# One decoder layer on one core: the order of its pieces dealt anew, ten halves by C on DVE, the first gate behind its softplus

## The chip, the cores and the metric

The kernel runs on one core of a Trainium2 chip. The metric is the device time of one execution in microseconds (us). Engines: PE (TensorE), DVE (VectorE), ACT (ScalarE), POOL (GpSimd) and SP (SyncE), which here only issues DMAs.

## The reference

32 sequences of 256 tokens of width 256 go through three blocks, each with a residual and a layer norm behind it.

```
# 1: state space block, d_inner 512, 16 states, scan restarts every 64 tokens
xc, res = split(x @ W_in.T + b_in)
u = silu(causal_conv3(xc) + conv_b)
dlt, Bm, Cm = split(u @ W_x.T)
delta = softplus(dlt @ W_dt.T + b_dt)
h[t] = exp(delta * A)[t] * h[t-1] + (delta * Bm * u)[t]     # per channel and state
y = sum over states of h * Cm
x = layernorm(x + (y * silu(res)) @ W_out.T + b_out)
# 2: cross attention, 16 heads of 16, keys and values from ctx_1024
x = layernorm(x + softmax(q k^T / 4) v @ w_o.T + b_o)
# 3: eight experts with fixed tokens (32 of each sequence to each)
x = layernorm(x + (silu(x @ w1) * (x @ w3)) @ w2)
```

Everything is float32.

## The kernel before

Blocks 1 and 2 run as one software pipeline over the 32 batches (sequences), block 3 follows over the eight experts. The change touches only the pipeline.

Each engine has a list of pieces (offset, function) which `run_steps` unrolls. An iteration has 16 slots. A piece with offset o runs for batch c in iteration c + o // 16, slot o % 16; within one slot the order is that of the list. So the offset says on each engine where a piece stands among the others, and the list says it only among pieces of one slot. There is no planner at run time: each engine executes its instructions in this order and waits on semaphores. SP's list is the order in which DMAs are issued, all on one queue; a wait of one holds up all behind it.

What happens to a batch:
- conv(m) and gate_proj(m), m = 0 to 3, on PE from xT. ACT evacuates (conv_evac, gate_evac), then in `silu` loads the table of Silu, makes u and the gate, and loads the table of Exp and Ln again.
- x_proj on PE gives delta's low-rank input and B and C, which xp_evac and bc_store put to DRAM; SP's bc_load replicates B and C over the partitions. dt_proj and ACT's softplus give delta. POOL's w_piece multiplies u by delta.
- SP's delta_store and w_store put both in DRAM, and replicate(part), part = 0 to 3, brings four tiles each of both back, replicated (8 DMAs of 128 KB). replicate(0) waits for both stores.
- The scan works in 16 tiles of 128 partitions x 4 states x 256 tokens. For tile t POOL makes dBu (L506, three buffers), ACT the decays in two halves of two states (L582, three PSUM banks), DVE scans each half (L764), and the states are multiplied by C: most by POOL in `h` (L516), the halves listed in HC_DVE by DVE. For these the scan is written to the PSUM bank, DVE's hC_piece multiplies it into h (L777), and clear_starts zeroes the first column of the bank (L787); only then is the half counted as scanned, which frees the bank for ACT and, for half 1, dBu's buffer for POOL.
- PE's state_sum(m) sums four tiles, DVE's gating multiplies by the gate, out_proj and residual(0) and norm(0) end block 1.
- Attention: k, q and v projections; `high` (ACT) and `low` (DVE) split q and k in two parts, store_parts stores them, load_stack(gr) reads them back stacked for four heads (eight DMAs of 64 KB in pieces of 1 KB, and a small one). scores, row_max (L829), max_transpose, scores_T, softmax_exp, pv and so on follow, one head a slot.

At the start SP loads the convolution's weights and the rows of biases; DVE multiplies both out (six products for w_conv, L733), casts the rows to `bias` (L738) and corrects them (L742). Then xT of batch 0 and ten weights are loaded; after the first of them SP waits until DVE is done. gate_proj(0) of the first batch waits for all ten.

Of the kernel before, what the change touches and what calls it, by code (L numbers as in the profile page):

```python
# [10 lines left out]
ALU = mybir.AluOpType  # L11
ACT = mybir.ActivationFunctionType
# [32 lines left out]
HC_DVE = [(1, 0), (1, 1), (4, 1), (5, 0), (5, 1), (6, 1), (8, 0), (9, 1), (10, 0), (10, 1), (14, 1)]  # L45
# [148 lines left out]
def mixers(nc, io, x2_dram, scratch, shared):  # L194
# [3 lines left out]
    with ExitStack() as ctx:  # L198
# [75 lines left out]
        def scores_T_bank(n):  # L274
# [4 lines left out]
        s_const = sem("weights_loaded")  # L279
        s_const_p = sem("const_set_pool")  # L280
# [49 lines left out]
        N_CONV = 6 + NDA + TAPS * KD  # L330
# [7 lines left out]
        def _(sp):  # L338
            sp.dma_start(w_xc.rearrange("p q t -> p (q t)"), io["w_xc"]).then_inc(s_conv_ld, 16)
            sp.dma_start(conv_rows, io["conv_rows"].partition_broadcast(P)).then_inc(s_conv_ld, 16)  # L340
            for tile, name in bias_parts:
                sp.dma_start(tile, io[name]).then_inc(s_bias_ld, 16)
# [107 lines left out]
            def store_x2T(b):  # L450
# [5 lines left out]
            run_steps([  # L456
                (O_K - 2, load_ctx),
                (O_Q + 3, store_parts(q_dram, s_q_hi, s_q_lo, s_q_dram)),
                (O_REP + 13, replicate(3)),
                *[(O_LD + 11 + 6 * e, load_expert(e, shared.load_w13)) for e in range(2)],  # L460
                *[(O_LD + 14 + 6 * e, load_expert(e, shared.load_w2)) for e in range(2)],
                (O_LD + 23, load_tokens),
                (O_K + 5, store_parts(k_dram, s_k_hi, s_k_lo, s_k_dram)),
                (O_SP + 2, w_store),
                (O_OUT, load_x_tok),
                (0 + 1, load_x),
                (O_SP + 2, delta_store),
                (O_XP + 2, bc_load),
                (O_REP + 1, replicate(0)),
                (O_REP + 7, replicate(2)),  # L470
                *[(O_LD + HG * gr - 2, load_stack(gr)) for gr in range(NG)],
                (O_X2T + 3, load_columns),
# [10 lines left out]
        @block.gpsimd  # L483
        def _(pool):
            nc.gpsimd.memset(k_st[4 * DK:SK].bitcast(F32), 0.0).then_inc(s_const_p, 1)
            pool.wait_ge(s_const_p, 1)
            nc.gpsimd.memset(q_st[4 * DK:SK].bitcast(F32), 0.0).then_inc(s_const_p, 1)
            pool.wait_ge(s_const_p, 2)
            nc.gpsimd.memset(v[:], 1.0).then_inc(s_const_p, 1)
            pool.wait_ge(s_const_p, 3)  # L490
            nc.gpsimd.memset(k_st[4 * DK:4 * DK + 2].bitcast(F32), 1.0).then_inc(s_const_p, 1)
            pool.wait_ge(s_const_v, N_SET)

            def w_piece(b):
# [25 lines left out]
            run_steps([  # L520
                *[(O_SCAN + t - 1, dBu_piece(t)) for t in range(NU)],
                (O_SP + 2, w_piece),
                *[(O_SCAN + t + 1, hC_piece(t)) for t in HC_POOL],
            ], B)

        @block.scalar
        def _(act):

            nc.scalar.preload_act_table_set(EXP_LN)
            act.wait_ge(s_bias_ld, 16 * len(bias_parts))  # L530
            nc.scalar.activation(a_neg[:], a_neg[:], ACT.Exp).then_inc(s_const_a, 1)
# [16 lines left out]

            def silu(b):
                act.wait_ge(s_conv, b.value(2, 2))  # L550
                nc.scalar.activation(u[:], u[:], ACT.Silu).then_inc(s_u, 1)
                act.wait_ge(s_gate, b.value(2, 2))
                nc.scalar.activation(gate[:, b.par], gate[:, b.par], ACT.Silu).then_inc(s_gsilu, 1)
                nc.scalar.preload_act_table_set(EXP_LN)

# [136 lines left out]
            def max_load(gr):  # L692
# [11 lines left out]
                *[(O_GATE + 4 * half + 2, gate_evac(half)) for half in range(2)],  # L704
                (O_K + 1, high(s_k_mm, s_k_hi, s_q_dram, 1)),
                (O_N2 + 3, store_x2),
                *[(O_SCAN + t - 1, decay(t, 0)) for t in range(NU)],
                *[(O_MT + HG * gr + 2, max_store(gr)) for gr in range(NG)],
                *[(O_MT + HG * gr + 3, max_load(gr)) for gr in range(NG)],
# [7 lines left out]
                (O_Q + 1, high(s_q_mm, s_q_hi, s_k_dram, 0)),  # L717
# [7 lines left out]
        def _(dve):  # L725
            nc.vector.memset(xT[:, :, 0:TAPS - 1], 0.0).then_inc(s_const_v, 1)
            nc.vector.memset(eps, EPS).then_inc(s_const_v, 1)
            for i in range(NDA):
                nc.vector.memset(dA[i][:], 0.0).then_inc(s_const_v, 1)
            dve.wait_ge(s_conv_ld, 32)  # L730
# [4 lines left out]
            dve.wait_ge(s_bias_ld, 16 * len(bias_parts))  # L735
            nc.vector.tensor_tensor(rows, rows, row_scales, ALU.mult).then_inc(s_const_v, 1)
            dve.wait_ge(s_const_v, N_CONV - 3)
            nc.vector.tensor_copy(bias[:], rows).then_inc(s_const_v, 1)  # L738
            dve.wait_ge(s_const_v, N_CONV - 2)

# [5 lines left out]
            dve.wait_ge(s_const_a, 1)  # L746
# [112 lines left out]
            def x1T_evac(b):  # L859
# [7 lines left out]
                (O_OF + 1, residual(1, s_of_mm, a_ps, s_r2, s_st2, s_mv2, s_ln2, s_x1, TT)),  # L867
# [3 lines left out]
                *[(O_ON + HG * gr + 1, head_norm(gr)) for gr in range(NG)],  # L871
                *[(O_SCAN + t, scan(t, 1)) for t in range(NU)],
# [9 lines left out]
        def _(pe):  # L882
# [20 lines left out]
            def gate_proj(m):  # L903
                def piece(b):
                    pe.wait_ge(s_xT, b.value(16, 16))
                    if m == 0 and not b.back(1):
                        pe.wait_ge(s_const, 16 * N_WEIGHTS)
                        pe.wait_ge(s_const_v, N_SET)
                        pe.wait_ge(s_const_p, 4)
                    if m % 2 == 0:  # L910
                        bank_f.wait_read(pe)
                        mm(f_ps[:], bias[32:36, m // 2 * P:(m // 2 + 1) * P], bias[32:36, BC:], True, False)
                    for k in range(KD):
                        i = mm(f_ps[:, m % 2], w_gate[:, k, m * P:(m + 1) * P], xT[:, k, TAPS - 1:], False,
                               m % 2 == 1 and k == KD - 1)
                    i.then_inc(s_gate_mm, 1)
                    bank_f.read_by(s_gate, 2, b, m // 2 + 1)
                return piece

            def x_proj(b):  # L920
                pe.wait_ge(s_u, b.value(1, 1))
# [16 lines left out]
            def state_sum(m):  # L938
                def piece(b):
                    n = b.value(NU, 4 * m)  # L940
                    pe.wait_ge(s_hC, b.value(len(HC_POOL), sum(t < 4 * m + 4 for t in HC_POOL)))
# [148 lines left out]
            def attn_out(tt):  # L1090
# [17 lines left out]
                *[(O_GATE + 4 * (m // 2), gate_proj(m)) for m in range(ND)],  # L1108
                (O_X1T, transpose(x_of, s_x1, TT, s_x1T_mm, s_x1T, bank_a, a_ps)),
                *[(O_DT, dt_proj(m)) for m in range(ND)],  # L1110
                *[(O_V, v_proj(tt)) for tt in range(TT)],
                *[(O_OF, attn_out(tt)) for tt in range(TT)],
# [318 lines left out]
```

## Time and profile before

| | |
|---|---|
| three runs | 2794.74 us median (2792.72 to 2795.35) |
| profiled execution | 2792.28 us, span 2790.5 us, mean granted clock of TensorE 0.955 |
| PE busy | 2424.6 us (87%) |
| DVE busy | 2140.0 us (77%) |
| POOL busy | 2074.5 us (74%), all of it in the pipeline of blocks 1 and 2 |
| ACT busy | 1802.9 us (65%) |
| DMA | 399.65 MB, mean 143 GB/s |

The span runs from the first to the last instruction. Busy shares are over the whole span; the pipeline ends at some 2270 us, so an engine's share there is higher. POOL has nothing to do in the last quarter.

### The profile page before, as it was taken

What the parts mean: (1) busy time and instruction counts of PE and PEld (TensorE: products, weight loads), DVE (VectorE), ACT (ScalarE), POOL (GpSimd) and SP (SyncE); (2) the same over time, 40 slices, a digit from 0 to 9 for tenths busy, and PEclk for the clock granted to TensorE, in tenths of its full rate; (3) what the DMA queues carried; (4) which work ended last, traced back from release to release, by engine and by line L of the source; (5) the groups of instructions that cost most, each with busy time, mean ns of one, the idle gap of its engine ahead of it and who ended that gap; (6) DMA issues with size and microseconds to landing.
All of it is one profiled execution on the core that took longest, in us unless ns stands there. A gap on an engine that the chain in (4) does not pass through costs nothing. (4 is left out here: it accounts for less than half of the span.)

```text
span 2790.5 us, 49779 instructions
## 1 busy us (share of the span) xinstructions
PE 2424.6 (87%) x14816; PEld 1660.6 (60%) x14816; DVE 2140.0 (77%) x3586; ACT 1802.9 (65%) x3972; POOL 2074.5 (74%) x968
## 2 busy tenths in 40 slices
PE   3578888888889898889889888898888879999998
PEld 2345666666666666666666666666665545555554
DVE  1778999999999999999999999999999832322332
ACT  1666777877888888777877787878777541211111
POOL 2999999999999999999999999999999500000000
PEclk8788999999999999999999999999998879999999
DMA  3456566666666666666666666666666360343221
GB/s 118 128 133 149 150 165 168 165 158 157 157 169 166 160 158 165 165 162 168 166 169 164 162 164 166 165 173 163 166 172 158 86 180 12 91 126 96 78 79 31
DMA packets 319323, 399.65 MB, mean 143 GB/s; under 512 B 115697, under 2 KB 256241, under 8 KB 314962
## 3 DMA queue, kind: packets, MB, share of 16 engines
q1 hardware_dynamic: 303698, 384.91, 53.5%
q10 hardware_dynamic: 15360, 11.55, 1.5%
q8 instruction: 124, 2.03, 0.3%
q14 instruction: 141, 1.16, 0.2%
HBM read 300.86 MB, written 94.37 MB: 142 GB/s over the span
## 5 line engine op out<-in xcount | busy, mean ns | idle before, releaser
L506 POOL TENSOR_TENSOR arena<-arena 128x1024 f32<-128x1024 f32 x512 | 1208.2, 2363 | 66.6 <-DMA arena<-w_dram 42.3
L582 ACT ACTIVATE dA_ps<-arena,a_neg 128x252 f32<-128x252 f32 x2048 | 868.7, 461 | 330.4 <-DVE dA_ps L787 172.0
L764 DVE TENSOR_TENSOR_SCAN arena<-dA_ps,arena 128x512 f32<-128x512 f32 x672 | 803.6, 1208 | 112.5 <-ACT dA_ps L582 88.0
L516 POOL TENSOR_TENSOR arena<-arena 128x1024 f32<-128x1024 f32 (+1 forms) x416 | 808.1, 1943 | 17.8 <-DVE arena L764 17.2
L764 DVE TENSOR_TENSOR_SCAN dA_ps<-dA_ps,arena 128x512 f32<-128x512 f32 x352 | 416.2, 1205 | 3.9 <-POOL arena L506 3.7
L887 PE MATMUL a_ps<-xT,w_conv 128*128 128x256 f32 x1536 | 369.8, 391 | 0.0
L829 DVE TENSOR_REDUCE mx<-s_ps 128x2 f32<-128x512 f32 x497 | 334.0, 672 | 23.2 <-PE s_ps L887 23.2
L887 PEld LDWEIGHTS a_ps<-xT,w_conv 128*128 128x128 f32 x1536 | 288.4, 194 | 54.1 <-issue 16.5
L887 PE MATMUL y_ps<-arena,sel 128*32 128x256 f32 x4096 | 257.5, 393 | 55.5 <-DVE m_rows L835 27.8
L640 ACT ACTIVATE probs<-st_ps 128x512 f32<-128x512 f32 x493 | 285.3, 579 | 29.7 <-PE st_ps L887 25.5
L887 PE MATMUL s_ps<-k_st,q_st 96*128 96x256 f32 x994 | 260.6, 344 | 43.7 <-DVE mx L829 28.0
L887 PE MATMUL st_ps<-q_st,k_st 96*128 96x256 f32 x986 | 221.9, 307 | 51.5 <-ACT probs L640 41.8
L777 DVE TENSOR_TENSOR arena<-dA_ps,arena 128x512 f32<-128x512 f32 x352 | 230.9, 677 | 4.4
L887 PEld LDWEIGHTS st_ps<-q_st,k_st 96*128 96x128 f32 x986 | 154.1, 194 | 120.1 <-issue 100.3
L887 PEld LDWEIGHTS s_ps<-k_st,q_st 96*128 96x128 f32 x994 | 166.7, 197 | 98.0 <-issue 59.4
L887 PEld LDWEIGHTS y_ps<-arena,sel 128*32 128x32 f32 x4096 | 127.9, 112 | 144.2 <-POOL arena L516 64.9
L1240 DVE TENSOR_TENSOR hT<-silu,u_ps 128x512 f32<-128x512 f32 x80 | 55.0, 688 | 193.7 <-PE u_ps L1311 160.9
L887 PE MATMUL a_ps<-bias 2*128 2x512 f32 (+2 forms) x192 | 93.3, 486 | 117.4 <-DVE parts L819 38.4
L1213 ACT ACTIVATE silu<-g_ps 128x512 f32<-128x512 f32 (+1 forms) x96 | 56.5, 596 | 210.0 <-PE g_ps L1311 209.9
L1311 PE MATMUL g_ps<-arena 128*128 128x512 f32 x384 | 181.7, 599 | 3.1 <-PEq L198 3.1
L1311 PE MATMUL u_ps<-arena 128*128 128x512 f32 x320 | 150.5, 592 | 0.0
L1329 PE MATMUL d_ps<-arena,hT 128*128 128x256 f32 x640 | 145.9, 383 | 0.0
(111 smaller groups left out, 3272.9 us busy)
## 6 DMA issues: line engine op xcount, KB each, us to landing
arena<-delta_dram SPq DMA_DIRECT2D x512, 128.0 KB, 2.8
arena<-w_dram SPq DMA_DIRECT2D x512, 128.0 KB, 3.2
arena<-bc_dram SPq DMA_DIRECT2D x128, 256.0 KB, 4.5
q_st<-q_parts_dram SPq DMA_DIRECT2D x512, 64.0 KB
k_st<-k_parts_dram SPq DMA_DIRECT2D x512, 64.0 KB
w_dram<-u SPq DMA_DIRECT2D x32, 512.0 KB, 2.8
delta_dram<-delta SPq DMA_DIRECT2D x32, 512.0 KB, 3.8
k_parts_dram<-parts SPq DMA_DIRECT2D x32, 512.0 KB, 4.0
```

Source lines behind the costliest of these rows:

```text
L506: pool.tensor_tensor(dBu[:, n % NB], w_r[:, n // RP % 2, t % RP].unsqueeze(1).to_broadcast([P, QS, L]), bc_r[:, b.par, 0], ALU.mult).then_ ...
L516: pool.tensor_tensor(h[:, n % NH, states], h[:, n % NH, states], bc_r[:, b.par, 1, states], ALU.mult).then_inc(s_hC, 1)
L582: last = nc.scalar.activation(dA[n % NDA][:, q, :, 1:], delta_r[:, n // (2 * RP) % 2, t % RP].rearrange("p (c t) -> p c t", t=CH)[:, :, 1: ...
L640: nc.scalar.activation(probs[:, n % NPROB], scores_T_bank(n), ACT.Exp, scale=float(DK) ** -0.5).then_inc(s_exp, 1)
L764: nc.vector.tensor_tensor_scan(dst, decays, dBu[:, n % NB, 2 * half:2 * half + 2].rearrange("p q t -> p (q t)"), 0.0, ALU.mult, ALU.add).t ...
L777: nc.vector.tensor_tensor(h[:, n % NH, 2 * half:2 * half + 2], state[:].rearrange("p q c t -> p q (c t)"), bc_r[:, b.par, 1, 2 * half:2 * ...
L829: nc.vector.tensor_reduce(mx[:, hd], scores_bank(b.value(H, hd)), AX.X, ALU.max).then_inc(s_max, 1)
L887: return nc.tensor.matmul(out, lhsT, rhs, start=first, stop=last)
L1213: nc.scalar.activation(dst, g_ps[i % 2][first:last], ACT.Silu).then_inc(f_silu, 1)
L1240: nc.vector.tensor_tensor(hT[first:last, i // 2, HALF * (i % 2):HALF * (i % 2 + 1)], silu[first:last, i % 2], ups[first:last], ALU.mult).t ...
L1311: ins = nc.tensor.matmul(ps[i % 2][:], w13[:, b.par, k, col:col + P], x2T[:, b.par, k, cols], start=(k == 0), stop=(k == KD - 1))
L1329: nc.tensor.matmul(d_ps[(2 * t + i) % ND_PS][:, 0:D], hT[:, k, tokens], w2[:, b.par, k], start=(k == 0), stop=False)
```

## The change

- HC_DVE has ten halves instead of eleven: tiles 1, 2, 4, 5, 6, 8, 9 and 14 with half 1, tile 10 with both. Before: tiles 1, 5 and 10 with both, 4, 6, 9 and 14 with half 1, 8 with half 0. So POOL has 15 pieces by C a batch, 8 of them of half a tile, instead of 13 with 5.
- The first batch's gate projections, their evacuation and silu come behind its softplus (offset O_SP + 2).
- Set-up: the rows of biases are loaded first, ACT converts them to `bias` instead of DVE, DVE does the six products behind the rows. Three weights (w_x, w_dt, w_gate) are loaded at once, with a semaphore of their own; x_proj of the first batch waits for these, and state_sum(0) for the others.
- The lists of SP, POOL, ACT, DVE and PE are ordered anew, and some offsets change by one.

```diff
-HC_DVE = [(1, 0), (1, 1), (4, 1), (5, 0), (5, 1), (6, 1), (8, 0), (9, 1), (10, 0), (10, 1), (14, 1)]
+HC_DVE = [(1, 1), (2, 1), (4, 1), (5, 1), (6, 1), (8, 1), (9, 1), (10, 0), (10, 1), (14, 1)]
...
+        front_weights = [(w_x[:], "w_x"), (w_dt[:], "w_dt"), (w_gate[:], "w_gate")]
         weights = [
-            (w_gate[:], "w_gate"), (w_x[:], "w_x"), (w_dt[:], "w_dt"), (sel[:], "sel"), (w_out[:], "w_out"),
+            (sel[:], "sel"), (w_out[:], "w_out"),
...
             def load_weights():
+                for tile, name in front_weights:
+                    sp.dma_start(tile, io[name]).then_inc(s_front, 16)
+                sp.wait_ge(s_const_v, N_SET)
                 for tile, name in weights:
                     sp.dma_start(tile, io[name]).then_inc(s_const, 16)
-                    sp.wait_ge(s_const_v, N_SET)
...
+                (O_REP + 13, replicate(3)),
+                *[(O_LD + 11 + 6 * e - 1, load_expert(e, shared.load_w13)) for e in range(2)],
+                *[(O_LD + 14 + 6 * e - 2, load_expert(e, shared.load_w2)) for e in range(2)],
+                (O_LD + 23, load_tokens),
+                (O_REP + 7, replicate(2)),
+                (O_K + 5, store_parts(k_dram, s_k_hi, s_k_lo, s_k_dram)),
                 (O_K - 2, load_ctx),
+                (O_SP + 2, delta_store),
                 (O_Q + 3, store_parts(q_dram, s_q_hi, s_q_lo, s_q_dram)),
...
-                (O_OUT, load_x_tok),
+                (O_OUT - 1, load_x_tok),
+                (O_X2T + 4, load_columns),
+                (0 + 1, load_x),
+                (O_XP + 2, bc_load),
                 (O_SP + 2, w_store),
                 (O_REP + 1, replicate(0)),
-                *[(O_LD + HG * gr - 2, load_stack(gr)) for gr in range(NG)],
+                *[(O_LD + HG * gr - 1, load_stack(gr)) for gr in range(NG)],
...
+            act.wait_ge(s_const_v, N_ROWS)
+            nc.scalar.activation(bias[:], rows, ACT.Copy).then_inc(s_const_a, 1)
...
+            def silu_gate(b):
+                act.wait_ge(s_gate, b.value(2, 2))
+                nc.scalar.activation(gate[:, b.par], gate[:, b.par], ACT.Silu).then_inc(s_gsilu, 1)
+
             def silu(b):
                 act.wait_ge(s_conv, b.value(2, 2))
                 nc.scalar.activation(u[:], u[:], ACT.Silu).then_inc(s_u, 1)
-                act.wait_ge(s_gate, b.value(2, 2))
-                nc.scalar.activation(gate[:, b.par], gate[:, b.par], ACT.Silu).then_inc(s_gsilu, 1)
+                if b.back(1):
+                    silu_gate(b)
                 nc.scalar.preload_act_table_set(EXP_LN)
+
+            def first_gate(b):
+                if not b.back(1):
+                    for half in range(2):
+                        gate_evac(half)(b)
+                    silu_gate(b)
+                    nc.scalar.preload_act_table_set(EXP_LN)
...
+                (O_SP + 2, first_gate),
...
-                (O_N2, norm(1, s_mv2, s_ln2, s_x2)),
+                (O_N2 - 1, norm(1, s_mv2, s_ln2, s_x2)),
...
-                (O_Q + 1, high(s_q_mm, s_q_hi, s_k_dram, 0)),
+                (O_Q, high(s_q_mm, s_q_hi, s_k_dram, 0)),
...
                 *[(O_SCAN + t, scan(t, 1)) for t in range(NU)],
+                *[(O_S + hd + 1, row_max(hd)) for hd in range(H)],
+                (O_Q + 1, low(s_q_hi, s_q_lo)),
                 *[(O_SCAN + t, hC_piece(t, half)) for t, half in HC_DVE],
-                *[(O_S + hd + 1, row_max(hd)) for hd in range(H)],
...
-                (O_Q + 1, low(s_q_hi, s_q_lo)),
...
-                    if m == 0 and not b.back(1):
-                        pe.wait_ge(s_const, 16 * N_WEIGHTS)
-                        pe.wait_ge(s_const_v, N_SET)
-                        pe.wait_ge(s_const_p, 4)
...
+            def first_gate(b):
+                if not b.back(1):
+                    for m in range(ND):
+                        gate_proj(m)(b)
...
             def x_proj(b):
+                if not b.back(1):
+                    pe.wait_ge(s_front, 16 * len(front_weights))
+                    pe.wait_ge(s_const_v, N_SET)
...
+                (O_SP + 2, first_gate),
```

## Rows read from the trace of the kernel before

**Rows 1.** Busy time of POOL in the second batch and in 28 later ones.
```profile
115.00:180.00 65.00, 63.64 (x30) 0.78 0.38 111
245.00:2119.00 1874.00, 1805.39 (x841) 0.98 0.65 164
```

**Rows 2.** Timeline of POOL: w_piece of batch 3 and of batch 31 (start, length).
```profile
245.39 2.36 POOL L497 TENSOR_TENSOR u<-u,delta 128x1024 f32<-128x1024 f32 x1 [0.29 <-ACT delta L572]
...
2119.09 2.35 POOL L497 TENSOR_TENSOR u<-u,delta 128x1024 f32<-128x1024 f32 x1 [0.16 <-ACT delta L572]
```

**Rows 3.** Groups of POOL's instructions in 245:2119 us (busy, mean ns, idle before).
```profile
L506 POOL TENSOR_TENSOR arena<-arena 128x1024 f32<-128x1024 f32 x449 | 1059.7, 2363 | 48.3 <-DMA arena<-w_dram 28.7 <-DVE dA_ps L787 18.7
L516 POOL TENSOR_TENSOR arena<-arena 128x1024 f32<-128x1024 f32 x224 | 529.2, 2362 | 15.8 <-DVE arena L764 15.2
L516 POOL TENSOR_TENSOR arena<-arena 128x512 f32<-128x512 f32 x140 | 177.9, 1270 | 0.0
```

**Rows 4.** Timeline of SP's queue of DMA issues in one steady batch.
```profile
770.22 0.36 SPq L419 DMA_DIRECT2D q_st<-q_parts_dram  x1
...
773.90 0.59 SPq L421 DMA_DIRECT2D q_st<-k_st  x1
...
780.38 1.74 SPq L363 DMA_DIRECT2D arena<-bc_dram  x4
...
784.80 0.34 SPq L371 DMA_DIRECT2D w_dram<-u  x1
...
789.49 0.33 SPq L398 DMA_DIRECT2D ctxT<-in_ctxT  x1
...
790.58 2.33 SPq L386 DMA_DIRECT2D arena<-delta_dram  x4
```

**Rows 5.** Timeline of ACT in that batch: first decay of the next.
```profile
799.50 1.66 ACT L582 ACTIVATE dA_ps<-arena,a_neg 128x252 f32<-128x252 f32 x4 [0.28 <-DMA arena<-w_dram]
```

**Rows 6.** Stretches of that batch; last three columns: granted clock, DMA share, GB/s.
```profile
772.00:781.00 9.00, 7.45 (x65) 4.94 (x56) 7.80 (x13) 8.76 (x17) 8.72 (x6) 1.00 0.47 62
781.00:786.00 5.00, 4.00 (x10) 2.96 (x11) 4.34 (x8) 4.96 (x10) 4.84 (x3) 0.66 0.99 211
786.00:789.00 3.00, 2.76 (x15) 2.19 (x14) 2.63 (x5) 2.38 (x6) 2.01 (x2) 1.00 0.91 339
789.00:791.00 2.00, 2.00 (x23) 1.37 (x25) 2.00 (x3) 1.56 (x5) 2.00 (x2) 1.00 0.33 53
793.00:798.00 5.00, 4.92 (x46) 3.40 (x39) 4.97 (x7) 4.44 (x12) 5.00 (x3) 1.00 1.01 238
```

**Rows 7.** Groups of DVE's instructions in 245:2119 us.
```profile
L777 DVE TENSOR_TENSOR arena<-dA_ps,arena 128x512 f32<-128x512 f32 x309 | 202.6, 676 | 3.8
L804 DVE TENSOR_TENSOR x_tok<-a_ps,x_tok 128x512 f32<-128x512 f32 x55 | 37.4, 680 | 37.5 <-PE a_ps L887 37.5
L787 DVE MEMSET dA_ps<- 128x8 f32 x308 | 15.2, 65 | 0.4
```

**Rows 8.** Timeline of all engines over the front.
```profile
15.73 5.49 PE L887 MATMUL a_ps<-xT,w_conv 128*128 128x256 f32 x12
...
30.93 0.76 PE L887 MATMUL f_ps<-bias 4*128 4x512 f32 x1 [9.71 <-issue]
...
35.12 2.76 PE L887 MATMUL a_ps<-xT,w_conv 128*128 128x256 f32 x12
...
46.88 0.60 ACT L538 ACTIVATE u<-a_ps 128x512 f32<-128x512 f32 x1 [2.00 <-PE a_ps L887]
...
49.75 1.04 ACT L553 ACTIVATE gate<-gate 128x1024 f32<-128x1024 f32 x1
...
59.10 0.43 SPq L367 DMA_DIRECT2D delta_dram<-delta  x1
...
64.33 1.71 SPq L386 DMA_DIRECT2D arena<-delta_dram  x4
...
70.61 2.45 ACT L582 ACTIVATE dA_ps<-arena,a_neg 128x252 f32<-128x252 f32 x6 [13.09 <-DMA arena<-w_dram]
```

More of the change, by code:

```diff
@@ L279, in mixers @@
         s_const = sem("weights_loaded")
+        s_front = sem("front_weights_loaded")
         s_const_p = sem("const_set_pool")
@@ L329, in mixers @@
         N_WEIGHTS = len(weights)
-        N_CONV = 6 + NDA + TAPS * KD
+        N_ROWS = 3 + NDA
+        N_CONV = 5 + NDA + TAPS * KD
         N_SET = N_CONV + 2
@@ L338, in _ @@
         def _(sp):
+            for tile, name in bias_parts:
+                sp.dma_start(tile, io[name]).then_inc(s_bias_ld, 16)
             sp.dma_start(w_xc.rearrange("p q t -> p (q t)"), io["w_xc"]).then_inc(s_conv_ld, 16)
             sp.dma_start(conv_rows, io["conv_rows"].partition_broadcast(P)).then_inc(s_conv_ld, 16)
-            for tile, name in bias_parts:
-                sp.dma_start(tile, io[name]).then_inc(s_bias_ld, 16)
             def load_weights():
+                for tile, name in front_weights:
+                    sp.dma_start(tile, io[name]).then_inc(s_front, 16)
+                sp.wait_ge(s_const_v, N_SET)
                 for tile, name in weights:
                     sp.dma_start(tile, io[name]).then_inc(s_const, 16)
-                    sp.wait_ge(s_const_v, N_SET)
                 sp.wait_ge(s_const_p, 4)
@@ L521, in _ @@
                 *[(O_SCAN + t - 1, dBu_piece(t)) for t in range(NU)],
+                *[(O_SCAN + t + 1, hC_piece(t)) for t in HC_POOL],
                 (O_SP + 2, w_piece),
-                *[(O_SCAN + t + 1, hC_piece(t)) for t in HC_POOL],
             ], B)
@@ L551, in silu, with later_gate_evac, piece @@
                 nc.scalar.activation(u[:], u[:], ACT.Silu).then_inc(s_u, 1)
-                act.wait_ge(s_gate, b.value(2, 2))
-                nc.scalar.activation(gate[:, b.par], gate[:, b.par], ACT.Silu).then_inc(s_gsilu, 1)
+                if b.back(1):
+                    silu_gate(b)
                 nc.scalar.preload_act_table_set(EXP_LN)
+            def first_gate(b):
[4 more added lines that the diff above has]
+                    nc.scalar.preload_act_table_set(EXP_LN)
+            def later_gate_evac(half):
+                def piece(b):
+                    if b.back(1):
+                        gate_evac(half)(b)
+                return piece
             def xp_evac(b):
@@ L703, in _ @@
                 (O_SILU, silu),
-                *[(O_GATE + 4 * half + 2, gate_evac(half)) for half in range(2)],
+                *[(O_GATE + 4 * half + 2, later_gate_evac(half)) for half in range(2)],
                 (O_K + 1, high(s_k_mm, s_k_hi, s_q_dram, 1)),
@@ L707, in _ @@
                 *[(O_SCAN + t - 1, decay(t, 0)) for t in range(NU)],
+                (O_SP + 2, first_gate),
+                *[(O_MT + HG * gr + 3, max_load(gr)) for gr in range(NG)],
                 *[(O_MT + HG * gr + 2, max_store(gr)) for gr in range(NG)],
-                *[(O_MT + HG * gr + 3, max_load(gr)) for gr in range(NG)],
                 (O_XP + 1, xp_evac),
                 *[(O_MT + HG * gr + 1, max_high(gr)) for gr in range(NG)],
-                (O_N2, norm(1, s_mv2, s_ln2, s_x2)),
+                (O_N2 - 1, norm(1, s_mv2, s_ln2, s_x2)),
                 *[(O_CONV + 4 * half + 3, conv_evac(half)) for half in range(2)],
@@ L729, in _ @@
                 nc.vector.memset(dA[i][:], 0.0).then_inc(s_const_v, 1)
+            dve.wait_ge(s_bias_ld, 16 * len(bias_parts))
+            nc.vector.tensor_tensor(rows, rows, row_scales, ALU.mult).then_inc(s_const_v, 1)
             dve.wait_ge(s_conv_ld, 32)
@@ L734, in _ @@
                                             conv_rows[:, tap * DI:(tap + 1) * DI], ALU.mult).then_inc(s_const_v, 1)
[L735 to L739, printed above, removed]
+            dve.wait_ge(s_const_a, 1)
             for first, last, cols in ((0, 96, BC), (96, P, 2 * BC)):
@@ L866, in _ @@
                 *[(O_SCAN + t, scan(t, 0)) for t in range(NU)],
-                (O_OF + 1, residual(1, s_of_mm, a_ps, s_r2, s_st2, s_mv2, s_ln2, s_x1, TT)),
                 (O_X1T + 1, x1T_evac),
@@ L918, in gate_proj, with later_gate, piece @@
                 return piece
+            def first_gate(b):
+                if not b.back(1):
+                    for m in range(ND):
+                        gate_proj(m)(b)
+            def later_gate(m):
+                def piece(b):
+                    if b.back(1):
+                        gate_proj(m)(b)
+                return piece
             def x_proj(b):
+                if not b.back(1):
+                    pe.wait_ge(s_front, 16 * len(front_weights))
+                    pe.wait_ge(s_const_v, N_SET)
                 pe.wait_ge(s_u, b.value(1, 1))
@@ L940, in piece @@
                     n = b.value(NU, 4 * m)
+                    if m == 0 and not b.back(1):
+                        pe.wait_ge(s_const, 16 * N_WEIGHTS)
+                        pe.wait_ge(s_const_p, 4)
                     pe.wait_ge(s_hC, b.value(len(HC_POOL), sum(t < 4 * m + 4 for t in HC_POOL)))
@@ L1107, in _ @@
                 *[(O_CONV + 2 * m, conv(m)) for m in range(ND)],
-                *[(O_GATE + 4 * (m // 2), gate_proj(m)) for m in range(ND)],
+                *[(O_GATE + 4 * (m // 2), later_gate(m)) for m in range(ND)],
+                (O_SP + 2, first_gate),
                 (O_X1T, transpose(x_of, s_x1, TT, s_x1T_mm, s_x1T, bank_a, a_ps)),
+                *[(O_OF, attn_out(tt)) for tt in range(TT)],
                 *[(O_DT, dt_proj(m)) for m in range(ND)],
                 *[(O_V, v_proj(tt)) for tt in range(TT)],
-                *[(O_OF, attn_out(tt)) for tt in range(TT)],
                 *[(O_OUT, out_proj(tt)) for tt in range(TT)],
```

13 lines of the change are left out of this document (2 added, 11 removed).

## The prediction

> **What bounds the kernel now.** I read the stretches of POOL first, then its groups with what ended their idle time, then SP's own queue, then the stretches by DMA share, and last the front. The w_piece of batch 3 starts at 245.39 and that of batch 31 at 2119.09 [rows 2]: 28 cycles of 66.92 us. POOL is busy 1805.39 of that stretch [rows 1], 64.48 us a cycle, so it idles 2.44. The reader should see in [rows 3] that 28.7 us of this idle time end with the landing of arena<-w_dram (1.0 a cycle), 18.7 with DVE's clearing of a bank (0.7) and 15.2 with a DVE scan (0.5). The first is the one that matters: it is the replication of delta and w for the first four tiles of a batch, replicate(0), and ACT's first decay waits for the same landing [rows 5]. So the cycle is a loop: landing of replicate(0), then POOL, ACT, DVE and PE with little slack for three quarters of a batch, softplus, w on POOL, the two stores, replicate(0), landing.
>
> The last part of the loop lies in SP's queue and is full of DMA. In the batch shown, stack(3) is issued from 770.22 to 774.49, SP then waits, bc_load goes at 780.38, w_store at 784.80, load_ctx at 789.49 (it waited for v_proj), replicate(0) at 790.58 [rows 4], and it has landed at 799.5 [rows 5]. The DMA engines are only 0.47 busy from 772 to 781, when stack(3) runs by itself at 62 GB/s. Then the share is 0.99 (bc), 0.91 (stores), 0.33, and 1.01 (replication) [rows 6]. Before bc_load there is room; behind it there is nearly none. The columns also show that a pure byte count misleads: the same 16 engines move 339/0.91 = 373 GB/s of busy time in the stores and 62/0.47 = 132 in the stack loads.
>
> **The change part by part.**
>
> *Order on each engine.* A piece's place is its offset modulo 16, then its place in the list. Only pieces of one slot can swap by the list. Going through the lists, on PE nothing swaps except the first batch's gate. On POOL only the length of hC pieces changes. On ACT norm(1) moves from slot 2 to 1, and the high part of q from 12 to 11. On DVE row_max and the low part of q go ahead of the hC pieces. On SP three orders change: bc_load now comes ahead of stack(3) (slots 11 and 11, before 11 and 10), delta_store ahead of w_store, and k's store behind replicate(2). So most of "dealt anew" is the same order written otherwise.
>
> *Ten halves instead of eleven.* POOL before: 8 full pieces and 5 halves a batch; after: 7 full and 8 halves (only tile 10 is wholly DVE's). That is 3 x 1.27 - 2.36 = +1.45 us by the means of [rows 3], +1.4 because successive instructions overlap by a few hundredths. POOL's own work becomes 64.5 + 1.4 = 65.9, which leaves 1.0 under the present cycle. It can take the place of the waits for DVE (1.2 a cycle), but not of the wait for the landing, behind which it begins. DVE loses one product and one clear: 0.68 + 0.07 = 0.74 us a batch [rows 7]. The other moves, (1,0) to (2,1) and (8,0) to (8,1), are the same work elsewhere. The clearing of half 1 frees dBu's buffer and of half 0 only a bank, so two tiles more hold dBu until DVE's product is done: between 0 and 2 x 0.68 = 1.4 for POOL. I take 0, as dBu waits for a bank only 0.7 a cycle in all.
>
> *bc_load ahead of stack(3).* This is the step I charge. stack(3) is nine DMAs, 4.3 us to issue [rows 4], and 0.47 x 9 = 4.2 us of all DMA engines [rows 6]. They move from the empty stretch to between bc_load and the stores. bc has its data until 786; the stack then takes until 790.2; the stores need 0.91 x 3 = 2.7 and a little, so they end at 793.1, not at about 789.3. ctx and q's store, issued while SP waits, take some 2.2 more (791 to 793 now), and the bulk of replicate(0), now 793 to 798, becomes 795.3 to 800.3: 2.3 later. From both sides: nothing, if bc_load comes earlier by as much or the landing was not the last thing awaited; 4.2, if none of the gaps fills. The gaps from 781 to 793 hold 0.05 + 0.27 + 1.34 = 1.7, of which the blocks above use nearly all, so I stay at 2.3. Queued behind on SP are delta_store, w_store, ctx, q's store and replicate(0); for the last POOL and ACT wait, and through decay(0) DVE. stack(3) itself, needed by the scores of head 12, lands as they start; its bound is 0 to 1 us of PE, and I take 0.
>
> As measured, the stack's 1 KB pieces cost the DMA engines 4.2 us for 0.5 MB. By the Trainium skill, "DMA: Bandwidth & Descriptors", section "Why small descriptors are slow (HBM only)", a packet has a fixed cost of about 3 cycles beside one per 32 bytes, which for 1 KB is 35 instead of 32, a tenth. By that rule the 0.5 MB would need an estimated 1.6 us at the stores' rate and would fit the gaps, which is the first rival below. The trace does not agree: 132 GB/s is far from a tenth below 373.
>
> *delta_store ahead of w_store.* In the steady batches it is issued behind the stack now and wins nothing. In the front it does (below).
>
> *The moves that I price together.* DVE's row maxima come up to 0.68 or 1.35 us sooner in nine slots. PE's maximum transposes wait for them, PE's out_proj follows, and DVE waits 37.5/28 = 1.3 a cycle for out_proj [rows 7]. Bounds 0 and 1.3; I take 0.3, a quarter, as only the group in that slot is on this path. norm(1) one slot earlier makes ACT wait for moments before a decay, q's high part earlier delays one exponential by 0.6; both fall where ACT waits for DVE anyway. Cost 0, bounds -0.5 to +0.6 a cycle.
>
> *The front.* Now PE stops after the first convolution block, because the first gate projection waits for all ten weights until 30.93 [rows 8]. After the change conv runs on: block 0 ends at 21.2 (its cold 5.49), block 1 takes 2.76 to 3.2, the evacuation and the bias product 1.4, blocks 2 and 3 5.6, so the second evacuation starts at 31.2 instead of 46.88: 15.7 less. The reordering of DVE's and ACT's set-up leaves PE's start where it is: the six products (3.7 us) now come last instead of the conversion, bounds -1 and +1, I take 0. delta_store no longer waits for w: both stores now start at 58.7 and 59.10, and replicate(0) goes at 64.33 [rows 8]; with delta gone 2.9 earlier the last landing comes 1.7 sooner. Bounds 0 and 2.9. Sum of the front -17.4. The gate that is put behind softplus costs PE about 5 us and ACT 0.6 x 2 + 1.3 + 1.04 + 1.3 = 4.8; they are covered by the 13.09 us in which ACT awaits the replication [rows 8]. Without that cover it would cost some 5.
>
> **The sum,** against the profiled execution's own 2792.28 (span 2790.5; it lies 2.46 under the median of the three runs, 2794.74):
> front -17.4; cycles 1 to 3, in which POOL's 30 instructions fill 63.64 of 65 us [rows 1] and no stack is loaded yet, 3 x 1.4 = +4.2; 28 cycles x (2.3 - 0.74 - 0.3) = 28 x 1.25 = +35.0. Together +21.8: 2814.1, and on the scale of the median 2816.5.
>
> **Rivals.**
> *The DMA shift is hidden, and the front decides (faster).* Place: replicate(0)'s landing. If stack(3) costs the loop less than about 0.6, the cycle is paced by POOL's 65.9 and what DVE still makes it wait, 66.5 say. For it: the landing is late by only 1.0 in the mean, and the batch has slack where bc_load waits for its store. Against: POOL, ACT and DVE all hang on that landing. Time: -17.4 + 4.2 - 28 x 0.4 = -24.4, so 2770. It decides from where the steady cycle grows by less than 0.27.
> *Break even.* The same with a cycle longer by 0.27 to 0.67, about 2795.
> *Both costs in full.* The stack takes its 4.2 and POOL's 1.4 isn't absorbed but for half: 28 x (4.2 - 0.74 + 0.7) = +116, less 13: 2897.
> *The front doesn't come.* Should the first gate or the weights end later than the replication, up to 5 of the 17.4 go; it stays inside the range of each case.
>
> **Chances.** Forecast 0.51 (its own range 2803 to 2850), hidden 0.29, break even 0.12, both in full 0.08. What a measurement of this kernel can tell from no change is about 0.2%, 5.6 us. Faster 0.29, same 0.12, slower 0.59. The range reaches down to the hidden case and leaves out most of the last: 2768 to 2862.
>
> **What would show it.** replicate(0) issued some 13 us behind bc_load instead of 10.2; stack(3) between bc_load and the stores; POOL's and ACT's wait for arena<-w_dram at 2 to 3 us a cycle while POOL's waits for DVE shrink; cycles of w_piece near 68.2; the first softplus some 16 us earlier. If the cycles are 66.9 or less the step on the DMA is wrong. If ACT's first decay isn't near 53, the front is.

## The result, and the profile after

The changed kernel takes 2828.29 us (median of 4 runs, 2825.39 to 2832.81) against 2795.05 for the kernel before in the same comparison. The ratio is 1.012, 95% interval 1.0102 to 1.0138. The profiled execution took 2826.22, against 2792.28: +33.9, where the forecast had +21.8.

The page's span line, then POOL in the two stretches of [rows 1] (us, busy and instructions, granted clock, DMA share, GB/s):

```profile
span 2824.4 us, 49751 instructions
```

```profile
115.00:180.00 65.00, 65.00 (x33) 0.84 0.45 128
245.00:2119.00 1874.00, 1808.74 (x882) 0.97 0.66 161
```

In the second batch's 65 us POOL now has no idle moment: its added work took the place of the 1.36 us that it idled there before. The w_piece of batch 3 and of batch 31, to be set beside [rows 2]:

```profile
231.93 2.34 POOL L502 TENSOR_TENSOR u<-u,delta 128x1024 f32<-128x1024 f32 x1
...
2137.63 2.37 POOL L502 TENSOR_TENSOR u<-u,delta 128x1024 f32<-128x1024 f32 x1 [0.25 <-ACT delta L596]
```

28 cycles of (2137.63 - 231.93)/28 = 68.06 us instead of 66.92. So the +33.9 divide as follows. The w_piece of batch 3 is 13.5 earlier, the 28 cycles are 32.0 longer, and from the w_piece of batch 31 to the end of the span 686.8 us pass instead of 671.4, 15.4 more.

POOL's groups in 245:2119 us, the answer to [rows 3]:

```profile
L511 POOL TENSOR_TENSOR arena<-arena 128x1024 f32<-128x1024 f32 x441 | 1041.7, 2362 | 58.8 <-DMA arena<-w_dram 57.3 <-DVE dA_ps L810 1.3
L521 POOL TENSOR_TENSOR arena<-arena 128x1024 f32<-128x1024 f32 x193 | 456.4, 2365 | 6.0 <-DVE arena L787 5.7
L521 POOL TENSOR_TENSOR arena<-arena 128x512 f32<-128x512 f32 x221 | 281.8, 1275 | 0.0
```

The waits for DVE (18.7 and 15.2) are down to 1.3 and 5.7; the wait for the landing of replicate(0) is up from 28.7 to 57.3, two us a cycle. POOL's own work is 1808.74 in 27.5 cycles, 65.7 instead of 64.5.

SP's issues in one steady batch, as in [rows 4], and ACT's first decay of the next batch, as in [rows 5]:

```profile
1046.60 2.50 SPq L368 DMA_DIRECT2D arena<-bc_dram  x4
...
1049.21 0.36 SPq L424 DMA_DIRECT2D q_st<-q_parts_dram  x1
...
1053.10 0.59 SPq L426 DMA_DIRECT2D q_st<-k_st  x1
...
1053.88 0.35 SPq L372 DMA_DIRECT2D delta_dram<-delta  x1
...
1054.41 0.34 SPq L376 DMA_DIRECT2D w_dram<-u  x1
...
1056.99 0.33 SPq L403 DMA_DIRECT2D ctxT<-in_ctxT  x1
...
1060.21 1.74 SPq L391 DMA_DIRECT2D arena<-delta_dram  x4
```

```profile
1067.28 1.66 ACT L606 ACTIVATE dA_ps<-arena,a_neg 128x252 f32<-128x252 f32 x4 [0.17 <-DMA arena<-w_dram]
```

stack(3) (1049.21 to 1053.69) stands between bc_load and the stores, and replicate(0) goes 13.6 us behind bc_load instead of 10.2; in the mean of the 30 batches from the third on it is 13.5 instead of 10.9. The stretches of that batch, as in [rows 6] (last columns: granted clock, DMA share, GB/s):

```profile
1038.00:1047.00 9.00, 7.44 (x73) 5.11 (x72) 7.81 (x13) 8.75 (x18) 9.00 (x5) 1.00 0.03 7
1047.00:1052.00 5.00, 3.64 (x19) 2.73 (x17) 4.59 (x9) 4.96 (x8) 5.00 (x4) 1.00 0.76 205
1052.00:1056.00 4.00, 2.56 (x10) 1.99 (x11) 3.96 (x7) 3.36 (x9) 3.94 (x3) 0.94 1.12 138
1056.00:1060.00 4.00, 4.00 (x28) 2.53 (x26) 2.99 (x5) 3.06 (x8) 4.00 (x3) 0.64 1.01 346
1062.00:1067.00 5.00, 4.88 (x33) 3.68 (x25) 5.00 (x8) 3.67 (x9) 4.07 (x2) 1.00 0.97 230
```

The stretch ahead of bc_load, 0.47 busy before, is now empty (0.03), and from 1052 to 1067 the DMA engines are hardly ever free. The four us from 1052 to 1056 belong almost wholly to stack(3), fully busy at 138 GB/s. (The share adds up the times of all packets; over 1.00, packets of one engine overlap.)

The front, as in [rows 8]:

```profile
16.10 7.97 PE L910 MATMUL a_ps<-xT,w_conv 128*128 128x256 f32 x24
...
25.25 5.45 PE L910 MATMUL a_ps<-xT,w_conv 128*128 128x256 f32 x24
...
30.73 0.60 ACT L545 ACTIVATE u<-a_ps 128x512 f32<-128x512 f32 x1 [6.02 <-PE a_ps L910]
...
41.85 0.34 SPq L372 DMA_DIRECT2D delta_dram<-delta  x1
...
42.66 3.78 PE L910 MATMUL f_ps<-xT,w_gate 128*128 128x256 f32 x8
...
47.96 2.79 SPq L391 DMA_DIRECT2D arena<-delta_dram  x4
...
53.64 1.06 ACT L558 ACTIVATE gate<-gate 128x1024 f32<-128x1024 f32 x1
...
56.01 2.45 ACT L606 ACTIVATE dA_ps<-arena,a_neg 128x252 f32<-128x252 f32 x6
```

The four convolution blocks run through, the second evacuation starts at 30.73 (46.88), and the decays start at 56.01 (70.61).

Four waits of the steady stretch (who waited for whom: us in total, times, longest). In the kernel before they were 7.1, 5.6, 37.5 and 11.1 us, so the first, second and fourth have grown much and the third little:

```profile
ACT rstd L616 <- DVE mean_var L836: 70.5, 54, 2.7
PE s_ps L910 <- DMA q_st<-k_st: 24.6, 27, 2.4
DVE x_tok L827 <- PE a_ps L910: 43.0, 28, 2.0
DVE mx L852 <- PE s_ps L910: 33.6, 36, 2.0
```

And the end of SP's queue in the pipeline, where the weights of expert 0 (L182) are now issued between the last two stack loads:

```profile
2275.47 0.59 SPq L426 DMA_DIRECT2D q_st<-k_st  x1
...
2276.10 2.05 SPq L182 DMA_DIRECT2D arena<-in_w  x4
...
2278.26 0.40 SPq L424 DMA_DIRECT2D q_st<-q_parts_dram  x1
...
2281.98 0.59 SPq L426 DMA_DIRECT2D q_st<-k_st  x1
```

### The profile page after: what moved, and what is told of

It reads as the page before. It is cut to its first block, busy times and chain, and to the rows that moved or that the text cites. A ratio compares the mean times of both kernels' runs of the same rounds, so it can differ in the third digit from the quotient of the medians.

```text
span 2824.4 us, 49751 instructions
## 1 busy us (share of the span) xinstructions
PE 2432.1 (86%) x14816; PEld 1675.6 (59%) x14816; DVE 2126.4 (75%) x3521; ACT 1813.5 (64%) x3975; POOL 2114.2 (75%) x1032
## 4 chain that ended last, share of the span: by engine, by line
POOL 37%; PE 29%; issue 16%; SPq 5%; DVE 5%; DMA 5%; ACT 2%; ACTq 0%; DVEq 0%; POOLq 0%
POOL arena L511 20%; POOL arena L521 17%; PE a_ps L910 7%; PE g_ps L1348 6%; PE d_ps L1366 5%; PE u_ps L1348 5%; SPq L424 2%; PE f_ps L910 2%; SPq L391 1%; DMA w_dram<-u 1%; PE y_ps L910 1%; DVE arena L787 1%; ACT dA_ps L606 1%; DVE mx L852 1%; DVE dA_ps L787 1%
## 5 line engine op out<-in xcount | busy, mean ns | idle before, releaser
L787 DVE TENSOR_TENSOR_SCAN arena<-dA_ps,arena 128x512 f32<-128x512 f32 x704 | 846.1, 1211 | 113.3 <-POOL arena L511 45.7
L521 POOL TENSOR_TENSOR arena<-arena 128x512 f32<-128x512 f32 (+1 forms) x480 | 855.4, 1782 | 8.1 <-DVE arena L787 7.6
L787 DVE TENSOR_TENSOR_SCAN dA_ps<-dA_ps,arena 128x512 f32<-128x512 f32 x320 | 383.8, 1208 | 4.5 <-ACT dA_ps L606 2.0
L910 PEld LDWEIGHTS a_ps<-xT,w_conv 128*128 128x128 f32 x1536 | 289.4, 194 | 54.6 <-issue 16.5
L800 DVE TENSOR_TENSOR arena<-dA_ps,arena 128x512 f32<-128x512 f32 x320 | 214.5, 679 | 0.6
```

The source lines that it names most:

```text
L787: nc.vector.tensor_tensor_scan(dst, decays, dBu[:, n % NB, 2 * half:2 * half + 2].rearrange("p q t -> p (q t)"), 0.0, ALU.mult, ALU.add).t ...
L800: nc.vector.tensor_tensor(h[:, n % NH, 2 * half:2 * half + 2], state[:].rearrange("p q c t -> p q (c t)"), bc_r[:, b.par, 1, 2 * half:2 * ...
L910: return nc.tensor.matmul(out, lhsT, rhs, start=first, stop=last)
```

## The experiments

Each is a kernel of its own, timed over five rounds beside the kernel before on the same chip. The kernel before had medians of 2794.6, 2793.0 and 2792.2 in the three comparisons. The last four kernels below were timed in the third comparison and are set against kernels of the second; by the ratios their differences come out 1 to 3 us larger than by the medians. "Cycle" is the mean distance of w_piece from batch 3 to batch 31, "tail" the time from the last w_piece to the end of the span, both in the profiled execution. That is a single one, up to 12.7 us from the median of its kernel, so cycles that differ by 0.1 or 0.2 tell nothing.

**The stack loads back ahead of bc_load, in the changed kernel.**

```diff
-                *[(O_LD + HG * gr - 1, load_stack(gr)) for gr in range(NG)],
+                *[(O_LD + HG * gr - 2, load_stack(gr)) for gr in range(NG)],
```

> The changed kernel with the stack loads at their old offset, so that stack(3) is issued ahead of bc_load again; all else as changed, the tail's order too. Theory (moved DMA): replicate(0) comes some 10 us behind bc_load again instead of 13.6, POOL's wait for arena<-w_dram falls from 2.0 to about 1 us a cycle, the cycle from 68.06 to 66.7 and the time by 28 x 1.4 = 38 to about 2790. Rival (POOL's 1.4 us of added work is what costs): cycle stays above 67.6 and the time above 2815.

Measured: 2809.77, ratio 1.0046 (1.0025 to 1.0068), cycle 67.44, tail 682.9. Half of what was expected: 18 us come back, and 0.6 of the cycle. The rival is not confirmed either. replicate(0) goes 11.5 us behind bc_load in the mean, and POOL waits 39.2 us for its landing. Something else in the lists cost the rest: the kernel with ACT's new list alone (below) has the same cycle, 67.43.

**The experts' weights later, in the changed kernel.**

```diff
-                *[(O_LD + 11 + 6 * e - 1, load_expert(e, shared.load_w13)) for e in range(2)],
-                *[(O_LD + 14 + 6 * e - 2, load_expert(e, shared.load_w2)) for e in range(2)],
+                *[(O_LD + 12 + 6 * e, load_expert(e, shared.load_w13)) for e in range(2)],
+                *[(O_LD + 14 + 6 * e, load_expert(e, shared.load_w2)) for e in range(2)],
```

> The changed kernel with the expert weights' loads moved behind the last batch's stack(3) in SP's queue (slot 12 instead of 10). Theory (tail): in the changed kernel w1 and w3 of expert 0 are issued ahead of the last batch's stack(3) and from w_piece of batch 31 to the end 686.8 us pass instead of 671.4; here about 672, time 15 lower, about 2813; cycles unchanged at 68.1. Rival (the longer tail comes from the other orders or from the norm's place): the time stays within 4 of 2828.

Measured: 2830.20, ratio 1.0117 (1.0089 to 1.0144). The tail is 676.5, 10.3 shorter, but the cycle is 68.44 in the profile, though nothing of a steady batch was changed. The time is what the rival said, the tail two thirds of what the theory said, and the cycles of this execution scatter from 66.9 to 70.7 us. Inconclusive, and tried again below in the faster kernel.

**Ten halves only, in the kernel before** (the new HC_DVE and nothing else).

> The kernel before with the ten halves only. Theory: POOL's 1.4 us a batch are absorbed by its waits for DVE (1.2 a cycle), DVE has 0.74 less, so the cycle stays within 0.3 of 66.9 and the time within 10 of 2795, rather above for the first three cycles (+4). Rival (POOL is the bound): 28 x 1.4 + 4 = +43, about 2838.

Measured: 2782.79, ratio 0.9953 (0.9935 to 0.9971), cycle 66.30. Better than either theory, and the sign is against the small loss that the first expected. POOL's largest group in this kernel:

```profile
L506 POOL TENSOR_TENSOR arena<-arena 128x1024 f32<-128x1024 f32 x453 | 1075.5, 2374 | 14.9 <-DMA arena<-w_dram 13.4 <-DVE dA_ps L787 1.3
```

Its wait for DVE's clearing is nearly gone (18.7 to 1.3), and half of the wait for the landing too (28.7 to 13.4). Fourteen of its 28 cycles behind batch 3 last between 65.6 and 65.9, and POOL's own work is 65.7 a cycle; in the kernel before none fell below 65.9.

**The front only, in the kernel before** (set-up, first gate behind softplus; lists and halves as before).

> The kernel before with the new set-up and the first gate behind its softplus, and nothing else. Theory: first w_piece at 42.0 instead of 56.4, all behind it unchanged: 14 less, about 2781. Rival (the start is given back in the first cycles, as the pipeline then stands in another phase): less than 6 saved.

Measured: 2778.64, ratio 0.9934 (0.9910 to 0.9958), first w_piece at 40.76, cycle 66.89, tail 672.1. The 16 us are kept to the end.

**Halves and front together, all lists as before.**

> The changed kernel with all five lists as before (the first gate's entries added): ten halves and the new front, nothing of the new orders. Theory (the orders alone cost): the gains of the front (-16) and of the ten halves (-12) add, about 2767, cycle 66.3. Rival (with the front the pipeline stands in another phase and the gains don't add): 2778 or more.

Measured: 2762.62, ratio 0.9881 (0.9856 to 0.9905), cycle 66.42, tail 672.5. The gains add (0.9953 x 0.9934 = 0.9887). So the new lists alone turn 2763 into 2828. Of these, the lists of PE and POOL leave the order within every slot as it was, so SP's, ACT's and DVE's are what is left.

The next three put one new list each on this kernel.

**DVE's new list.**

```diff
-                *[(O_SCAN + t, hC_piece(t, half)) for t, half in HC_DVE],
                 *[(O_S + hd + 1, row_max(hd)) for hd in range(H)],
+                (O_Q + 1, low(s_q_hi, s_q_lo)),
+                *[(O_SCAN + t, hC_piece(t, half)) for t, half in HC_DVE],
```

> As the kernel with halves and front only, plus the changed list of DVE (row_max and q's low part ahead of the products by C, residual(1) behind head_norm). Theory (ACT's list is the second culprit): cycle within 0.3 of 66.3, time within 8 of the kernel with halves and front only. Rival (the products put later hold the banks and POOL's states): +1 a cycle, +28.

(residual(1) moves in the list too, but neither it nor the low part of q passes another piece of its slot; only the row maxima really moved.)

Measured: 2755.61, ratio 0.9856 (0.9830 to 0.9881), cycle 66.22. That is 7 us below the kernel without it in the same comparison, with overlapping intervals, so the gain is not clear of noise. It has the lowest median of the study, well below the kernel before and the changed one.

**ACT's new list.**

```diff
-                (O_N2, norm(1, s_mv2, s_ln2, s_x2)),
+                (O_N2 - 1, norm(1, s_mv2, s_ln2, s_x2)),
...
-                (O_Q + 1, high(s_q_mm, s_q_hi, s_k_dram, 0)),
+                (O_Q, high(s_q_mm, s_q_hi, s_k_dram, 0)),
```

> As the kernel with halves and front only, plus the changed list of ACT (norm(1) in slot 1, q's high part in slot 11). Theory: norm(1) makes ACT wait for the moments some 2.5 us a cycle as in the changed kernel (70.5 us in all), with decays and exponentials queued behind it; cycle up by about 1.1 to 67.4, time +30. Rival (ACT has that slack, as its waits for DVE shrink by as much): within 8.

Measured: 2788.58, ratio 0.9988 (0.9968 to 1.0009), cycle 67.43: +26. The waits of its steady stretch:

```profile
ACT rstd L616 <- DVE mean_var L836: 70.0, 55, 2.7
ACT dA_ps L606 <- DVE arena L787: 28.0, 73, 1.1
PE st_ps L910 <- ACT probs L664: 37.4, 27, 1.6
POOL arena L511 <- DMA arena<-w_dram: 39.4, 27, 3.1
```

and three of the kernel without the new list:

```profile
ACT dA_ps L606 <- DVE arena L787: 87.5, 117, 1.9
POOL arena L511 <- DMA arena<-w_dram: 19.0, 17, 2.5
DVE mx L852 <- PE s_ps L910: 8.0, 11, 2.4
```

ACT waits 70.0 us for the moments, 2.5 a cycle, instead of 7.4, with a decay and an exponential behind it. Its waits for DVE's scans fall from 87.5 to 28.0 at the same time, so most of the new wait took the place of an old one, as the rival had it; the cycle is 1.0 longer all the same. ACT now waits longer for PE's v_proj (46.6 instead of 27.4). The landing of replicate(0) is awaited 39.4 instead of 19.0, and replicate(0) goes 11.8 us behind bc_load instead of 11.0 in the mean. How the delay gets from the one place to the other was not followed. norm(1) and q's high part weren't tried apart; the wait speaks for norm(1).

**SP's new list.**

> As the kernel with halves and front only, plus the changed list of SP. Theory: replicate(0) 13.6 us behind bc_load instead of 10.2, POOL's wait for the landing up to 2 us a cycle, cycle +0.6 to +1.7, and 10 us more behind the last w_piece from the experts' weights: time +28 to +55. Rival (stack(3) is harmless and the other orders are what costs): within 8.

Measured: 2829.25, ratio 1.0125 (1.0101 to 1.0149), cycle 68.26, tail 688.9: +66.6, above the theory's upper end. replicate(0) goes 13.7 us behind bc_load in the mean, and POOL waits 60.1 us for its landing.

**Only stack(3) behind bc_load.**

```diff
-                *[(O_LD + HG * gr - 2, load_stack(gr)) for gr in range(NG)],
+                *[(O_LD + HG * gr - 2, load_stack(gr)) for gr in range(NG - 1)],
+                (O_LD + HG * 3 - 1, load_stack(3)),
```

(The experts' weights are one slot later too, so that they stay behind the last stack(3).)

> As the kernel with halves and front only (2762.6), but stack(3) behind bc_load in SP's queue, nothing else of SP's new list, and the experts' weights kept behind the last stack(3). Theory (the prediction's step alone): replicate(0) some 13 us behind bc_load, cycle up from 66.4 by 1.2 to 1.8, time +35 to +50. Rival (x_tok, k's store, or delta_store ahead of w_store carry it): within 8 of 2763.

Measured: 2808.62, ratio 1.0048 (1.0030 to 1.0066), cycle 68.16, tail 670.3: +46. replicate(0) comes 13.5 us behind bc_load in the mean of 30 batches, and 11.0 in the kernel with halves and front only. Its waits (the new line shifts the numbers by one):

```profile
PE s_ps L911 <- DMA q_st<-k_st: 48.2, 46, 2.2
POOL arena L512 <- DMA arena<-w_dram: 47.3, 31, 3.7
DVE mx L853 <- PE s_ps L911: 32.4, 35, 2.7
```

POOL waits 47.3 for the landing instead of 19.0. PE waits 48.2 us for stacks, or 1.7 a cycle, instead of 5.3, and behind it DVE's row maxima wait 32.4 instead of 8.0. Sorted by their distance from the last bc_load, 24.2 us of the 48.2 lie 8 to 12 us behind it, where the scores need stack(3), and 22.2 lie 24 to 28 us behind it, where they need stack(0) of the next batch, which is issued behind the late replicate(0).

**Only the experts' weights ahead of the last stack(3).**

```diff
-                *[(O_LD + 11 + 6 * e, load_expert(e, shared.load_w13)) for e in range(2)],
+                *[(O_LD + 10 + 6 * e, load_expert(e, shared.load_w13)) for e in range(2)],
```

> As the kernel with halves and front only, but w1 and w3 of the experts one slot earlier, so that they are issued ahead of the last batch's stack(3), as in the changed kernel. Theory (tail): cycles unchanged at 66.4, from the last w_piece to the end some 687 us instead of 672.5, time +10 to +16. Rival: the tail stays, +0 to +4.

Measured: 2771.14, ratio 0.9920 (0.9904 to 0.9935), cycle 66.24, tail 682.7: +8.5 by the medians, +10.9 by the ratios, +10.2 by the tails. The tails of all kernels bear it out: with the weights ahead of the last stack(3) they are 682.7 to 688.9 (this one, the changed one, and those with the stack back and with SP's new list), with the weights behind it 670.3 to 678.7. The same numbers show that a tail is only good to some 8 us.

**Eleven halves, spread: (12, 1) added to the fastest.**

> As the best so far (halves, front, DVE's new list, 2755.6), with (12, 1) added: eleven halves over ten tiles. Theory (banks: what the ten halves brought is the spreading, since with both halves of a tile on DVE ACT waits for banks): DVE has 0.74 more and POOL 1.1 less a cycle; POOL's own work falls from 65.6 to 64.5 and the cycle to 65.8, time -10. Rival (DVE's load is what counts): cycle above 66.6, time +10 or more.

Measured: 2774.18, ratio 0.9931 (0.9913 to 0.9949), cycle 66.73: +19, the rival's numbers. POOL's wait for the landing is 35.3. In the fastest kernel it is

```profile
POOL arena L511 <- DMA arena<-w_dram: 11.1, 15, 2.4
```

so POOL's smaller work buys only a longer wait. That DVE's 0.74 is what counts isn't shown, though: the next kernel puts the same half on DVE without adding one, and loses as much.

**Ten halves, none double: (10, 0) moved to (12, 1).**

> As the best so far, with (10, 0) moved to (12, 1): ten halves on ten tiles, none double. Theory (banks): ACT's waits for cleared banks fall further, POOL has one more short piece split (16 pieces, 10 of them halves: 0.2 more a cycle), the cycle stays within 0.3 of 66.2. Rival (POOL paces every cycle at 65.6 already): exactly the 0.2 come on top, time +5.

Measured: 2776.71, ratio 0.9943 (0.9925 to 0.9961), cycle 66.61, +21. Neither theory's number. The cycle is 0.4 longer with the same number of halves, so where they stand matters; why (12, 1) is a bad place is open. This place alone could also account for the +19 of the kernel above. Both kernels with it have DVE's m_rows awaited more by PE's state_sum (49.4 and 54.0 us against 39.4 in the fastest).

## Why the prediction was right, step by step

- **stack(3) between bc_load and the stores.** Right in place and in the delay, too high in what it costs. Taken: replicate(0) 2.3 later, and the cycle 2.3 longer. Measured, by itself: 2.5 later (13.5 against 11.0), and +46 us, 1.65 a cycle by the medians and 1.74 by the profiles. That +46 holds something the prediction put at 0: PE's waits for stacks. The one for stack(3), bound 1 us, is 0.9 a cycle; the one for stack(0) behind the late replicate(0), 0.8 a cycle, had no term. How the +46 divide between these and the landing was not tried.
- **The rest of SP's list.** The prediction names bc_load, delta_store and k's store. It passes over x_tok, which moved from between k's store and replicate(2) to ahead of stack(1) and replicate(1), and the experts' weights. By the times the rest costs another 12 without the weights (66.6 - 46.0 - 8.5). The profiles hardly show it in the steady cycle (68.26 with the whole list, 68.16 with stack(3) alone) and more in the tail (688.9, against 682.7 with the weights alone). Which of delta_store, k's store and x_tok has it was not tried.
- **Ten halves.** Taken: POOL's 1.4 absorbed, DVE's 0.74 a gain, +4.2 in the ramp, in all -16.5. Measured: -12 in the kernel before, -16 with the front. Right, and the profile shows the absorption: the waits for DVE are gone.
- **DVE's list.** Taken: -0.3 a cycle, 8.4 in all. Measured: -7, not clear of noise.
- **The front and the first three cycles.** Taken: -17.4 and +4.2, so -13.2 at the w_piece of batch 3. Measured there: -13.5. The parts were both too large and offset each other, which is luck: the first w_piece is 14.4 earlier, and from it to that of batch 3 pass 190.0 us instead of 189.0. The front alone, with delta_store still behind w_store, brings -16.0. The second evacuation came at 30.73, forecast 31.2. What followed gave some of it back: x_proj and the two parts of dt_proj took 2.78, 2.04 and 1.91 us instead of 1.97, 1.10 and 1.03, at the lower clock (last section). The 1.7 for delta_store ahead of w_store don't show: POOL's first dBu comes 13.4 us behind the first w_piece with SP's new list, and 13.2 without it. And the first gate used up its cover: its eight matmuls took 3.78 us a pair of blocks (1.99 for eight at the full clock), ACT had its silu from 53.64 to 54.70 and then 1.28 us of table load, and began the decays at 56.01, where the prediction wanted them near 53. POOL had its data and started at 55.62.
- **ACT's list: the step that failed.** It was put at 0 with an upper bound of 0.6 a cycle, since both moves "fall where ACT waits for DVE anyway". Measured: +26, some 0.93 a cycle. The slack was there, and most of it was spent as forecast (ACT's waits for DVE's scans fell by 59.5 us, its wait for the moments grew by 62.6), but the cycle did not stay as it was: ACT waited longer for v_proj (19.2 us more) and for the landing (45.2 instead of 36.3), and POOL for the landing (39.4 instead of 19.0). How the moved norm leads to these waits is open, and so is the share of q's high part.
- **The tail.** The prediction had no term for it. The weights' slot came to be that of the last stack(3), and the list puts them first. 10 us in a kernel of its own, 15.4 in the changed one.
- **Not additive.** The parts sum to -30.4 - 7 + 26 + 66.6 = +55, and the changed kernel has +33. Part of one wait hides behind the other; which part was not taken apart. That is also why moving the stacks back in the changed kernel gave 18 instead of 46.

On the scale of the median the forecast was 2816.5, with a range of its own of 2803 to 2850, and the median is 2828.29. So +21.8 came out near +33.9 with two terms missing (+26, +10) and 22 us of overlap that hid most of that. The cycle in particular, forecast 68.17 and measured 68.06, is close by luck: the parts by themselves give -0.50 (halves and front), -0.20 (DVE), +1.01 (ACT) and +1.84 (SP), 2.15 in all, and together they cost 1.14. Without this overlap, which the prediction didn't foresee, the cycle would have come out near 69.1.

The rivals: the hidden DMA is refuted (stack(3) behind bc_load costs 46 us by itself, and POOL waits 47 to 60 us for the landing), and with it the break-even case. The full sum of both costs was too much. Of the front 3 us didn't come.

The prediction set the stack's 132 GB/s beside the rule of the Trainium skill, "DMA: Bandwidth & Descriptors", section "Why small descriptors are slow (HBM only)", and blamed the 1 KB pieces. The moved stack again kept the DMA engines fully busy at 138 GB/s, so as a price for the stack the rule stays wrong. But the size of the pieces is not the reason, as the last section shows.

## What to carry to other kernels

In a software pipeline that is a loop, look for the stretch where the one queue is full, and count what a reordering moves into it, above all if what is moved came out of an empty stretch. An engine's idle time is not free to be spent at another place of its order: here 2.2 us more of one wait a cycle replaced 2.1 us of another and still cost 0.9. And after changing an offset by one, look at the last iteration too, where pieces that run once meet the regular ones.

## What the runs showed of the hardware

The stack loads moved 62/0.47 = 132 GB/s [rows 6] and 138/1.12 = 123 after the change per busy time of the DMA engines, the stores of delta and w, in pieces of 4 KB, 373 and 343. That factor of nearly 3 is what made stack(3) expensive. It doesn't come from the stack's pieces of 1 KB: q's store has pieces of 1 KB too, and in the us in which it runs almost alone the engines move 368/1.04 = 354 GB/s (columns as in [rows 6]):

```profile
1060.00:1061.00 1.00, 1.00 (x18) 0.68 (x18) 1.00 (x2) 1.00 (x4) 1.00 (x1) 1.00 1.04 368
```

Nor is it that the stack is loaded and not stored: in the kernel before, the load of batch 0's xT, also in pieces of 1 KB, has packets of 0.046 us in the mean (8 to 10 us), as q's store has, and the stack loads have 0.140 (773 to 775 us). Packets of 4 KB take 0.162 us (10 to 12 us), so 1 KB by itself takes 0.046 and as a fourth of a larger piece 0.041, an eighth less. For these other transfers the rule of the Trainium skill, "DMA: Bandwidth & Descriptors", section "Why small descriptors are slow (HBM only)", a tenth at 1 KB, does about agree. What sets the stack loads apart in the source is that each writes 16 partitions, four pieces to each, where xT is written to 128; whether that is the reason was not tried.

The queue worked in order of issue: the stores were issued at 1053.88 and 1054.41, and the rate rose from 138 to 346 GB/s only behind 1056.

TensorE lost its clock in the pauses of the front. The stretch from 25 to 31 us, the second half of the convolution, has a granted clock of 1.00, and its 24 instructions take 5.45. PE then waited for the evacuation, the silu, xp and softplus, with only short work between, and the stretches from 37 to 42 and, with the first gate, from 42 to 52 have 0.50, the lower of the two levels (1.2 of 2.4 GHz). In the kernel before, x_proj and dt_proj ran from 49.9 to 54.6 us at 1.00. Columns: busy time and instructions of PE, granted clock, DMA share, GB/s. The third and fourth line are the kernel before's, the others the changed kernel's:

```profile
25.00:31.00 6.00, 5.70 (x25) 1.00 0.00 0
37.00:42.00 5.00, 3.79 (x9) 0.50 0.53 118
...
49.90:52.00 2.10, 1.97 (x8) 1.00 0.00 0
52.50:55.00 2.50, 1.97 (x8) 1.00 0.05 13
...
16.00:24.00 8.00, 8.00 (x25) 1.00 0.65 218
42.00:52.00 10.00, 8.91 (x18) 0.50 0.69 208
```

The first 24 instructions of the convolution took 7.97 us, though the stretch from 16 to 24 is shown at 1.00 as well. The 1.00 is no measurement up to 21.25 us, where the trace's first record of the clock begins; a stretch without a record is shown at 1.00. The instructions start 0.43 us apart up to there and 0.22 apart behind it, the ratio of the two levels, so the first twelve ran at the lower one.
